# State scans: dt brought to the decay buffer by DMA, where TensorE spread it through PSUM

## The chip, the cores and the metric

The kernel runs on one core of one Trainium2 chip. The metric is the device time of one execution in microseconds (us), lower is better. The core has five engines with a queue of their own each: PE (TensorE, matmuls), DVE (VectorE), ACT (ScalarE), POOL (GpSimd) and SP (SyncE, which here only issues DMAs). ACT can issue DMAs too. Each queue is worked off in order; an instruction that waits for a semaphore holds up all that is queued behind it on its engine.

## The reference

A decoder of two layers over 4 sequences of 512 tokens with 512 features. What matters here are the two state-space (Mamba) mixers, `_L0_attn_ref` with 1024 channels and `_L1_xattn_ref` with 512, both with 16 states per channel:

```python
dt = jax.nn.softplus(jnp.einsum('blr,dr->bld', ts, dt_proj_w) + dt_proj_b)
A = -jnp.exp(A_log)

def step(h, inp):
    dt_t, B_t, C_t, x_t = inp
    dA = jnp.exp(dt_t[:, :, None] * A[None])
    h = dA * h + (dt_t * x_t)[:, :, None] * B_t[:, None, :]
    y = jnp.einsum('bdn,bn->bd', h, C_t)
    return (h, y)
...
x = _layernorm(x + _L0_attn_ref(x, ...))
x = _layernorm(x + _L0_xattn_ref(x, ...))
x = _layernorm(x + _L0_ffn_ref(x, ...))
x = _layernorm(x + _L1_attn_ref(x, ...))
x = _layernorm(x + _L1_xattn_ref(ctx_1024, x, ...))
x = _layernorm(x + _L1_ffn_ref(x, ...))
```

So every channel has one dt per token, and 16 decays dA = exp(dt * A), one for each state. Between the mixers stand a feed-forward net with 2048 hidden features (FFN) and a mixture of experts (MoE).

## The kernel before

Features lie on the 128 partitions, tokens (T = 512) along the free dimension. The sequences run one after another; the first `nc.Fori` body is repeated three times, and the last sequence has a copy of its own.

**A block of the scan.** `hidden_and_scan` handles 32 channels at a time, all with 16 states: 4 partition groups of 32 channels by 4 states (GRP) along the free dimension, so one block is a tile of 128 x 2048. A layer of 1024 channels has 32 blocks, one of 512 has 16. Per block s:

- PE, `spread_dt(s)` (L787): dt of 32 channels stands on 32 partitions. One float32 matmul with the constant `headmean` (four 32x32 identities side by side, divided by 16) copies it, over 16, to all 128 partitions of PSUM bank 0, `dt_bank`.
- ACT, `decays(s)` (L881): four exponentials read `dt_bank`, each with its own column of `rate` (A, multiplied by 16 at the start) as scale, and write the four quarters of the decay buffer `k.da[s % 2]`, 128 x 511 each. They wait for the matmul and, for the buffer, for the scan of block s - 2.
- PE, `spread_dtx(s)` (L799): the same spread for dt * x, into PSUM bank 1.
- DVE, `inputs(s)` (L912): dt * x times B, 128 x 2048, reads bank 1. `scan(s)` (L921): the recurrence over 2048 elements in one instruction; it waits for the decays and the inputs.
- POOL (L996): the states times C. PE, `reduce_quad` (L808): sums over the states, once per four blocks.

In the instruction records each of these float32 matmuls is two records (x2).

**What runs beside the scan.** The same function computes a hidden layer at the same time, one tile of 128 hidden features per step, and a step of the loop also holds one block of the scan. It is called in three ways:

- *first* (once, 32 blocks): no hidden layer. Beside the scan of the first sequence the weights are split into two bfloat16 parts (`WeightSplitter`): SP loads a slot of 768 KB (L211), ACT rounds it to the high part (L222), and the low part comes from DVE (L226) for every third slot, and for the others from PE (`rest_part`, L197 and L198) with a copy out of PSUM by ACT (`take_rest`, L203); SP then stores both parts (L214). 9 slots are handled in 4 steps; there are 4 buffers.
- *ffn* (4 times, 16 blocks of the second mixer, 16 tiles): gate, up and down products on PE (L258, L261, L262 are the three bfloat16 parts of one product), tanh on ACT (L888), the rest on DVE (L931, L939, L947, L244, L961).
- *moe* (3 times with 32 blocks of the next sequence's first mixer, 33 tiles; the fourth time without a scan).

**Order on the engines.** It is written out by hand. In a step of the loop PE has: `spread_dtx(step + 1)`, `spread_dt(step + 2)`, which waits until the decays of block step + 1 have read `dt_bank`, then gate and up of tile step + 1, the split's `rest_part`, `reduce_quad`, and a piece of the down product. ACT has: `decays(step + 1)`, tanh of tile step + 1, then the split's copies of the step. DVE has: `scan(step)`, the split's low part, `inputs(step + 1)`, and the tile's work. Ahead of the loop PE has `spread_dt(0)`, `spread_dtx(0)`, `gate(0)` (which waits for DVE's `xsplit`, four L244), `spread_dt(1)` and `up(0)`.

## Time and profile before

| | |
|---|---|
| device time, median of 3 runs | 4366.92 us (4363.65 to 4374.26) |
| device time of the profiled execution | 4378.06 us |
| its span, first to last instruction | 4376.3 us |
| PE busy | 3563.2 us, 81% |
| DVE busy | 3345.3 us, 76% |
| ACT busy | 1374.1 us, 31% |
| POOL busy | 1285.7 us, 29% |
| spread of dt and the decays, all of 192 blocks: PE L787 / ACT L881 busy | 232.5 / 463.2 us |
| mean granted TensorE clock | 0.884 of full speed |

The stretches with a scan in them are *first* (100 to 470 us), four times *ffn* (the first from 653 to 833 us) and three times *moe* (the first from 1118 to 1485 us). Read the busy shares with care. PE and DVE are both near full in some stretches, and an instruction counts as busy while it is held up by another engine. PE works on several row groups at once: matmuls of 32 rows that stand one behind the other in its queue can run together, and their busy times then cover the same stretch. What a stage costs is decided by the engine that has no idle time there, and by the waits that end last.

### The profile page before, as it was taken

Reading aid. Unit: us, or ns where it says so; the run is one execution under the profiler, and the core shown is the slowest. Engines: PE = TensorE matmul, PEld = TensorE weight load, DVE = VectorE, ACT = ScalarE, POOL = GpSimd, SP = SyncE. Lnnn points to the kernel's source line nnn. Section 1 sums busy time; section 2 is a strip of 40 time slices with the busy share of each in tenths; the row PEclk is TensorE's granted clock in tenths of the full one; section 3 lists DMA queues with packets and bytes.
Section 4 is the critical chain, followed back from the end, with each engine's and each line's share of the span. In section 5 each row is a group of like instructions: output and inputs, shape, how many; then the busy total and the mean of one; then the engine's idle time right before and its main releaser. Section 6 shows DMA issues by size and latency. Waiting matters only on the chain. (4 is left out here: it accounts for less than half of the span.)

```text
span 4376.3 us, 40273 instructions
## 1 busy us (share of the span) xinstructions
PE 3563.2 (81%) x14967; PEld 1484.2 (34%) x14967; DVE 3345.3 (76%) x2914; ACT 1374.1 (31%) x2022; POOL 1285.7 (29%) x452
## 2 busy tenths in 40 slices
PE   5777759887899859887899858978799967974898
PEld 1222233324333333323333333323333333321444
DVE  5998469777899768778799858868699868867444
ACT  4666333124322233214322233213422143221101
POOL 1543204332244203342244303333144312432000
PEclk9888879898899979989799978979799988986899
DMA  4888402221122302122122301122122311210222
GB/s 152 301 316 307 152 21 79 69 77 58 58 73 80 109 24 72 65 82 71 51 73 73 116 32 65 65 75 84 36 73 78 110 47 52 79 58 15 72 101 75
DMA packets 72917, 393.38 MB, mean 90 GB/s; under 512 B 8080, under 2 KB 8208, under 8 KB 70288
## 3 DMA queue, kind: packets, MB, share of 16 engines
q1 hardware_dynamic: 69264, 384.44, 25.1%
q10 hardware_dynamic: 3456, 6.29, 0.4%
q8 instruction: 126, 2.06, 0.2%
q14 instruction: 71, 0.58, 0.1%
HBM read 320.45 MB, written 70.25 MB: 89 GB/s over the span
## 5 line engine op out<-in xcount | busy, mean ns | idle before, releaser
L261 PE MATMUL ps<-r,ring 128*128 128x512 bf16 (+2 forms) x2040 | 801.2, 393 | 0.0
L996 POOL TENSOR_TENSOR hh<-hh,bc 128x2048 f32<-128x2048 f32 x72 | 336.9, 4679 | 1108.8 <-DVE hh L921 1108.8
L258 PE MATMUL ps<-r,ring 128*128 128x512 bf16 (+2 forms) x1384 | 557.5, 403 | 127.0 <-DVE xc L961 38.3
L258 PE MATMUL ps<-xr,ring 128*128 128x512 bf16 x1568 | 620.7, 396 | 5.5 <-DVE r L244 5.5
L262 PE MATMUL ps<-xr,ring 128*128 128x512 bf16 x1568 | 618.2, 394 | 0.0
L262 PE MATMUL ps<-r,ring 128*128 128x512 bf16 (+2 forms) x1384 | 556.4, 403 | 0.0
L881 ACT ACTIVATE da<-ps,params_sb 128x511 f32<-128x511 f32 x768 | 463.2, 690 | 72.7 <-PE ps L787 33.9
L996 POOL TENSOR_TENSOR bc<-bc 128x2048 f32<-128x2048 f32 x64 | 298.0, 4656 | 375.7 <-DVE bc L921 375.7
L996 POOL TENSOR_TENSOR r<-r,bc 128x2048 f32<-128x2048 f32 x56 | 261.8, 4674 | 327.8 <-DVE r L921 327.8
L921 DVE TENSOR_TENSOR_SCAN hh<-da,hh 128x2048 f32<-128x2048 f32 x72 | 326.7, 4538 | 1.5
L888 ACT ACTIVATE row<-ps 128x512 f32<-128x512 f32 x100 | 59.7, 597 | 754.5 <-PE ps L262 754.5
L921 DVE TENSOR_TENSOR_SCAN bc<-da,bc 128x2048 f32<-128x2048 f32 x64 | 289.6, 4525 | 0.5
L787 PE MATMUL ps<-r,squares_sb 32*128 32x512 f32 x384 | 232.5, 687 | 64.4 <-PEq L2026 49.6
L261 PEld LDWEIGHTS ps<-r,ring 128*128 128x128 bf16 (+2 forms) x2040 | 200.5, 98 | 248.7 <-issue 28.9
L258 PEld LDWEIGHTS ps<-r,ring 128*128 128x128 bf16 (+2 forms) x1384 | 136.8, 99 | 403.5 <-issue 265.9
L961 DVE TENSOR_TENSOR xc<-xc,ps 128x512 f32<-128x512 f32 x176 | 119.6, 680 | 198.9 <-PE ps L262 198.9
L258 PEld LDWEIGHTS ps<-xr,ring 128*128 128x128 bf16 x1568 | 153.5, 98 | 315.2 <-issue 141.5
L921 DVE TENSOR_TENSOR_SCAN r<-da,r 128x2048 f32<-128x2048 f32 x56 | 253.0, 4517 | 0.6
L888 ACT ACTIVATE r<-ps 128x512 f32<-128x512 f32 x96 | 57.3, 597 | 584.8 <-PE ps L262 584.8
L262 PEld LDWEIGHTS ps<-xr,ring 128*128 128x128 bf16 x1568 | 152.4, 97 | 211.5 <-issue 14.4
L197 PE MATMUL ps<-r,squares_sb 128*128 128x512 f32 x282 | 180.6, 727 | 53.1 <-ACT ring L222 20.3
L258 PE MATMUL ps<-bc,ring 128*128 128x512 bf16 (+2 forms) x320 | 139.2, 435 | 102.3 <-DMA ring<-wsplit 38.7
(240 smaller groups left out, 6486.9 us busy)
## 6 DMA issues: line engine op xcount, KB each, us to landing
ring<-wsplit SPq DMA_DIRECT2D x304, 768.0 KB, 4.2
r<-wstream SPq DMA_DIRECT2D x76, 768.0 KB, 7.4
wsplit<-ring SPq DMA_DIRECT2D x58, 768.0 KB, 4.9
wsplit<-r SPq DMA_DIRECT2D x18, 768.0 KB, 5.7
r<-xT SPq DMA_DIRECT2D x7, 1024.0 KB, 8.8
r<-gates_dram SPq DMA_DIRECT2D x3, 2048.0 KB, 8.3
bc<-guwT SPq DMA_DIRECT2D x4, 1024.0 KB, 12.1
out<-xr SPq DMA_DIRECT2D x4, 1024.0 KB, 7.0
```

The source lines that it names most:

```text
L197: pe.matmul(self.banks[:, c, :], ident, self.whole[n % SPLIT_RING][:, at], start=True, stop=False)
L258: mm = pe.matmul(out, w_hi, x_hi, start=start, stop=False)
L261: pe.matmul(out, w_hi, x_lo, start=False, stop=False)
L262: return pe.matmul(out, w_lo, x_hi, start=False, stop=stop)
L787: pe.matmul(dt_bank, k.headmean[at, :], dt[at, s // 4, :], start=True, stop=True).then_inc(dt_mm, 1)
L881: a = act.activation(k.da[s % 2][:, n, 1:T], dt_bank[:, 1:T], ACT.Exp, scale=rate[:, GRP * s + n:GRP * s + n + 1])
L888: act.activation(t2[jt % 2], gate_bank(jt), ACT.Tanh, scale=0.5).then_inc(th, 1)
L921: dve.tensor_tensor_scan(states(s), k.da[s % 2][:, :, :].rearrange("p n t -> p (n t)"), states(s), 0.0, ALU.mult, ALU.add).then_inc(scanne ...
L961: dve.tensor_tensor(k.xc[:, m, :], k.xc[:, m, :], down_bank(p), ALU.add).then_inc(taken, 1)
L996: pool.tensor_tensor(quartet(s), quartet(s), k.out_rows, ALU.mult).then_inc(read, 1)
```

## The change

dt reaches the four partition groups by DMA. A new `fetch(s)` on ACT's queue issues four DMAs (L871 of the changed kernel), each from the 32 partitions of dt to one group of 32 partitions in the first quarter of `k.da[s % 2]`, 32 x 511 float32 (65 KB). The four exponentials (L878) read that quarter; the one that overwrites it comes last, and waits until the other three have read it. `spread_dt`, its matmuls, the waits between it and the decays, and `dt_bank` go. The factor 16 in the rates goes with them.

`fetch(s)` for s >= 2 waits for the scan of block s - 2, as the decays did before, since the buffer is free only then. It stands in step s - 2, behind the decays and the tanh, and ahead of the split's copies. `fetch(0)` and `fetch(1)` stand at the start.

```diff
-        dt_mm, dtx_mm, decay = [sem(n) for n in ("dt_mm", "dtx_mm", "decay")]
+        dtx_mm, decay, others = [sem(n) for n in ("dtx_mm", "decay", "others")]
+        dt_in = [sem(f"dt_in{i}") for i in range(2)]
...
-            def spread_dt(s):
-
-                if s >= 1:
-                    pe.wait_ge(decay, s)
-                at = slice(32 * (s % 4), 32 * (s % 4) + 32)
-                pe.matmul(dt_bank, k.headmean[at, :], dt[at, s // 4, :], start=True, stop=True).then_inc(dt_mm, 1)
...
             if blocks:
-                spread_dt(0)
                 spread_dtx(0)
             if tiles:
                 pe.wait_ge(xsplit, KM)
                 gate(0)
-            if blocks:
-                spread_dt(1)
...
                     spread_dtx(step + 1)
-                if step + 2 < blocks:
-                    spread_dt(step + 2)
...
-            def decays(s):
-                act.wait_ge(dt_mm, s + 1)
+            def fetch(s):
+
                 if s >= 2:
                     act.wait_ge(scanned, s - 1)
-                for n in range(GRP):
-                    a = act.activation(k.da[s % 2][:, n, 1:T], dt_bank[:, 1:T], ACT.Exp, scale=rate[:, GRP * s + n:GRP * s + n + 1])
+                rows = dt[32 * (s % 4):32 * (s % 4) + 32, s // 4, 1:T]
+                for g in range(4):
+                    act.dma_start(k.da[s % 2][32 * g:32 * g + 32, 0, 1:T], rows).then_inc(dt_in[s % 2], 16)
+
+            def decays(s):
+                act.wait_ge(dt_in[s % 2], 64 * (s // 2 + 1))
+                for n in (1, 2, 3, 0):
+                    if n == 0:
+                        act.wait_ge(others, s + 1)
+                    a = act.activation(k.da[s % 2][:, n, 1:T], k.da[s % 2][:, 0, 1:T], ACT.Exp,
+                                       scale=rate[:, GRP * s + n:GRP * s + n + 1])
+                    if n == 3:
+                        a.then_inc(others, 1)
                 a.then_inc(decay, 1)
...
             if blocks:
+                fetch(0)
+                fetch(1)
                 decays(0)
...
                 if step + 1 < tiles:
                     gate_tanh(step + 1)
+                if step + 2 < blocks:
+                    fetch(step + 2)
                 for n, late in zip_longest(split_now(step), split_now(step, 2)):
...
-            dve.tensor_scalar(k.a0, k.a0, -16.0, None, ALU.mult)
-            dve.tensor_scalar(k.a1, k.a1, -16.0, None, ALU.mult).then_inc(neg, 1)
+            dve.tensor_scalar(k.a0, k.a0, -1.0, None, ALU.mult)
+            dve.tensor_scalar(k.a1, k.a1, -1.0, None, ALU.mult).then_inc(neg, 1)
```

ACT's queue in *first*, around step 3. L203 is `take_rest`, L222 the high part of a slot. Before:

```order
L881 ACTIVATE da<-ps,params_sb 128x511 [waits first_scanned,first_dt_mm]
L881 ACTIVATE da<-ps,params_sb 128x511 x3
L203 ACTIVATE ring<-ps 128x1536 [waits first_rest]
L222 ACTIVATE ring<-r 128x1536 [waits first_stored2,first_landed2]
L203 ACTIVATE ring<-ps 128x1536 [waits first_rest]
L222 ACTIVATE r<-r 128x1536 [waits first_stored3,first_landed3]
L222 ACTIVATE ring<-r 128x1536 [waits first_stored0,first_landed0]
```

With the change, at the same place:

```order
L878 ACTIVATE da<-da,params_sb 128x511 [waits first_dt_in0]
L878 ACTIVATE da<-da,params_sb 128x511 x2
L878 ACTIVATE da<-da,params_sb 128x511 [waits first_others]
L871 DMA da<-r 32x511 [waits first_scanned]
L871 DMA da<-r 32x511 x3
L203 ACTIVATE ring<-ps 128x1536 [waits first_rest]
L222 ACTIVATE ring<-r 128x1536 [waits first_stored2,first_landed2]
L203 ACTIVATE ring<-ps 128x1536 [waits first_rest]
L222 ACTIVATE r<-r 128x1536 [waits first_stored3,first_landed3]
L222 ACTIVATE ring<-r 128x1536 [waits first_stored0,first_landed0]
```

The wait for a scan has moved from ahead of the decays to behind them, and it is now one for the scan of this step (3), not of the one before (2). The five copies of the split stand behind it.

PE's queue in *first*, one step. Before:

```order
L799 MATMUL ps<-dtx_now,squares_sb 128x512 [waits first_dtx_in,first_inp]
L787 MATMUL ps<-r,squares_sb 128x512 [waits first_decay]
L197 MATMUL ps<-r,squares_sb 128x512 [waits first_low_act,first_high]
L198 MATMUL ps<-ring,r 128x512
L197 MATMUL ps<-r,squares_sb 128x512
```

With the change:

```order
L793 MATMUL ps<-dtx_now,squares_sb 128x512 [waits first_dtx_in,first_inp]
L197 MATMUL ps<-r,squares_sb 128x512 [waits first_low_act,first_high]
L198 MATMUL ps<-ring,r 128x512
L197 MATMUL ps<-r,squares_sb 128x512
```

L787 is gone, and with it PE's wait for ACT's decays ahead of the split's products.

PE's queue at the start of *ffn*; the semaphores there are used again and carry the names of their first use (`first_stored3` is `xsplit`, `first_landed2` is `decay`). Before, with the nine products between left out as they do not change:

```order
L787 MATMUL ps<-r,squares_sb 128x512
L799 MATMUL ps<-r,squares_sb 128x512
L258 MATMUL ps<-xr,ring 128x512 [waits w_landed0,first_stored3]
...
L262 MATMUL ps<-xr,ring 128x512
L787 MATMUL ps<-r,squares_sb 128x512 [waits first_landed2]
L258 MATMUL ps<-xr,ring 128x512 [waits w_landed0]
```

With the change:

```order
L793 MATMUL ps<-r,squares_sb 128x512
L258 MATMUL ps<-xr,ring 128x512 [waits w_landed0,first_stored3]
...
L262 MATMUL ps<-xr,ring 128x512
L258 MATMUL ps<-xr,ring 128x512 [waits w_landed0]
```

`spread_dt(0)` ahead of `spread_dtx(0)` and `spread_dt(1)` between gate and up of tile 0 are gone.

## Rows read from the trace of the kernel before

**Rows 1.** Windows: the first ffn and moe; us, busy per engine, PEclk, DMA, GB/s.
```profile
655.00:850.00 195.00, 177.17 (x799) 70.20 (x798) 170.27 (x120) 53.60 (x90) 74.78 (x17) 0.96 0.23 77
1120.00:1485.00 365.00, 341.34 (x1571) 128.67 (x1570) 347.81 (x258) 95.10 (x161) 147.02 (x32) 0.98 0.23 76
```

**Rows 2.** Groups by line: busy us, mean ns of one, idle before and releaser.
```profile
L881 ACT ACTIVATE da<-ps,params_sb 128x511 f32<-128x511 f32 x768 | 463.2, 690 | 72.7 <-PE ps L787 33.9 <-DVE bc L921 20.0 <-DVE r L921 14.1
L787 PE MATMUL ps<-r,squares_sb 32*128 32x512 f32 x384 | 232.5, 687 | 64.4 <-PEq L2026 49.6 <-ACT da L881 9.3 <-PEq L421 5.4
...
L1448 ACT ACTIVATE da<-r 128x511 f32<-128x511 f32 x32 | 17.0, 614 | 0.0
```

**Rows 3.** Timeline in moe, PE: start us, duration us; a pair of spreads.
```profile
1383.89 0.69 PE L799 MATMUL ps<-dtx_now,squares_sb 32*128 32x512 f32 x1
...
1383.89 0.69 PE L787 MATMUL ps<-r,squares_sb 32*128 32x512 f32 x1
...
1384.95 0.40 PE L258 MATMUL ps<-xr,ring 128*128 128x512 bf16 x1
```

**Rows 4.** Timeline near the end of ffn, PE: a spread of dtx alone.
```profile
801.58 1.12 PE L799 MATMUL ps<-r,squares_sb 32*128 32x512 f32 x2
```

**Rows 5.** Timeline in moe: decays of block 74, and the scan of block 74.
```profile
1388.59 2.42 ACT L881 ACTIVATE da<-ps,params_sb 128x511 f32<-128x511 f32 x4 [0.17 <-DVE hh L921]
...
1404.93 4.42 DVE L921 TENSOR_TENSOR_SCAN bc<-da,bc 128x2048 f32<-128x2048 f32 x1
```

**Rows 6.** Timeline at the start of the first ffn, PE and DVE.
```profile
653.37 2.50 DVE L244 TENSOR_TENSOR r<-xr 128x512 bf16<-128x512 f32 x4 [1.88 <-PEq L2026]
...
657.05 0.61 PE L258 MATMUL ps<-xr,ring 128*128 128x512 bf16 x1
...
662.28 1.23 PE L787 MATMUL ps<-r,squares_sb 32*128 32x512 f32 x2
...
663.44 0.40 PE L258 MATMUL ps<-xr,ring 128*128 128x512 bf16 x1
...
667.37 2.29 DVE L912 TENSOR_TENSOR hh<-ps,bc 128x2048 f32<-128x2048 f32 x1 [3.39 <-PE ps L799]
```

**Rows 7.** Timeline at the start of the first moe, DVE.
```profile
1132.20 2.29 DVE L912 TENSOR_TENSOR hh<-ps,bc 128x2048 f32<-128x2048 f32 x1 [2.89 <-PE ps L799]
```

**Rows 8.** The DMAs that ACT issues before: issue ns min/median/max, and landing.
```profile
L1460 ACTq DMA_DIRECT2D gates_dram<-r x12: 326/326/353, 975.6 to 2997.7; - x12
...
DMA to landing us min/median/max: 2.0/2.0/5.3
```

**Rows 9.** Timeline in first, steps 3 and 4, DVE.
```profile
140.67 1.73 DVE L226 TENSOR_TENSOR ring<-r,ring 128x1536 bf16<-128x1536 f32 x1
142.32 2.28 DVE L912 TENSOR_TENSOR r<-ps,bc 128x2048 f32<-128x2048 f32 x1
144.70 6.37 DVE L921 TENSOR_TENSOR_SCAN r<-da,r 128x2048 f32<-128x2048 f32 x1
151.92 5.40 DVE L226 TENSOR_TENSOR ring<-r,ring 128x1536 bf16<-128x1536 f32 x1 [0.85 <-ACT ring L222]
...
187.84 6.36 DVE L921 TENSOR_TENSOR_SCAN bc<-da,bc 128x2048 f32<-128x2048 f32 x1
```

**Rows 10.** The same stretch, POOL and ACT.
```profile
151.15 4.56 POOL L996 TENSOR_TENSOR r<-r,bc 128x2048 f32<-128x2048 f32 x1 [4.36 <-DVE r L921]
...
143.87 1.47 ACT L222 ACTIVATE ring<-r 128x1536 bf16<-128x1536 f32 x1
```

**Rows 11.** Timeline in first, second half: PE, ACT, and two scans four steps apart.
```profile
349.88 4.42 DVE L921 TENSOR_TENSOR_SCAN r<-da,r 128x2048 f32<-128x2048 f32 x1
...
352.77 2.07 PE L787 MATMUL ps<-r,squares_sb 32*128 32x512 f32 x2 [2.28 <-ACT da L881]
...
360.25 1.45 ACT L203 ACTIVATE ring<-ps 128x1536 bf16<-128x1536 f32 x1 [6.17 <-PE ps L198]
...
396.12 4.41 DVE L921 TENSOR_TENSOR_SCAN bc<-da,bc 128x2048 f32<-128x2048 f32 x1
```

2 lines of the change are left out of this document (1 added, 1 removed).

## The prediction, made before the changed kernel was run

> **What bounds the kernel now.** I read the windows by stage first, then the groups by line, then the timeline of one step in each kind of stage. In the first ffn and moe windows DVE is busy 170 of 195 us and 348 of 365, and PE 177 and 341 [rows 1]: both look full, so either could be the bound, and the 232.5 us that PE is busy with the spread of dt [rows 2] look like up to 5% of the time. The timeline says otherwise. The spreads of dtx and of dt stand next to each other in PE's queue and use different 32-row groups of the array. In moe both start at 1383.89, and the next product starts at 1384.95, 1.06 us later [rows 3]. At the end of ffn a spread of dtx that stands alone takes 1.12 us [rows 4]. The pair costs what one costs. Within the loop, then, the dt spread is nearly free on PE, and it is DVE's queue of scan, inputs and tile work that sets the step of ffn and moe.
>
> **Part 1, the spread leaves PE in the loop of ffn and moe.** By rows 3 against rows 4 the gain per step is about 0, at most some 0.4 us in the few steps where the two spreads do not start together. DVE would hide even that. I take 0 us. Ends: 0, and a gain of some 20 us if 0.2 us of each of the 112 later steps of PE (of 160) were on the path.
>
> **Part 2, ACT gets the DMAs and a wait.** Per block: four issues at 0.33 us if a 32-row issue costs what a 128-row issue of ACT costs [rows 8], and perhaps a third of that if it goes by rows; I take 1.0 us for four and call it f, with 0.4 to 1.4 as ends. The data lands 2.0 us after the last issue in quiet, 5.3 us beside a big load [rows 8]. The four exponentials take 2.42 us [rows 5]; the last now also waits for the third to finish, some 0.1 us. In moe the decays of block 74 start at 1388.59 and are done at 1391.0, and the scan that needs them starts at 1404.93 [rows 5]: 13.9 us in hand. The new chain adds f + 2.0 to 5.3 us + 0.1, so 3.1 to 6.8 us. Behind the waiting instructions on ACT stands only the tanh of the next tile, which is needed after that same scan. Cost in the loop of ffn and moe: 0 us; if the 13.9 us were not there, each step would pay the 3 us or more, 160 times.
>
> The exponentials now read SBUF. The one line of ACT that does so at this shape takes 614 ns, against 690 from PSUM [rows 2]: 192 x 4 x 0.076 = 58 us less on ACT, beside other work. The Trainium skill says the opposite (Perfetto Trace Analysis, Optimizing Scalar/DVE Operations): ScalarE's access overhead is about 93 ns on SBUF and 51 on PSUM, which by that page would be 768 x 0.042 = 32 us more. As ACT has slack in most stages, the sum is the same by either.
>
> **Part 3, the start of ffn and moe.** Here PE is late. `inputs(1)` waits 3.39 us for PE in ffn [rows 6] and 2.89 us in moe [rows 7]. Ahead of it on PE stand dt(0), dtx(0), gate(0), dt(1), up(0), dtx(1). Without dt(0), gate(0) can start when `xsplit` is done at 653.37 + 2.50 = 655.87, where it started at 657.05 [rows 6]: 1.2 us. Without dt(1), up(0) follows at once: 663.44 - 662.28 = 1.2 us [rows 6]. Some comes back: the products take 0.61 us before and 0.40 us after the clock has risen [rows 6], and if it rises no sooner, three or four of the up products run at the slow level, 0.2 us each. Net 1.7 us for ffn. In moe `xsplit` comes later behind the first `dtx_now`, so I take 1.4 us. Bounds: 0 and the whole idle time, 3.39 and 2.89 us. The decays of block 0 come from the DMA now: eight issues are 2f, the fourth lands 0.75f + 2.0 us after the start, and scan 0 moves by less than 1 us either way. Its end is still ahead of the new start of `inputs(1)`. DVE has no idle time in the rest of the loop, so what it gains here it keeps until the end of the stage, whose tail hangs on the last scan. Gain: 4 x 1.7 + 3 x 1.4 = 11 us (0 to 22).
>
> **Part 4, first.** Here ACT's order matters. DVE and POOL exclude each other for some of these instructions. Scan 4 starts at 144.70 and takes 6.37 us [rows 9], where 4.42 is normal [rows 5], since POOL is still at work; and the low part at 151.92 takes 5.40 us where the one at 140.67, which came before POOL's instruction, takes 1.73 [rows 9]. POOL started at 151.15 and ended at 155.71 [rows 10], and the low part ended 1.6 us after that. So it counts whether a low part is ready at once when a scan ends. Before, ACT ran ahead: it did the high part during the scan. Now the split's copies of step s stand behind `fetch(s + 2)`, which waits for the end of scan s. A low part that needs the high part of the same step (two of the three in four steps) can start f + 1.35 + 1.4 = 3.8 us after the scan's end at the soonest; a copy takes 1.47 us [rows 10]. By then POOL has the ports until 4.6 us. So both such steps look like the one at 151.92. From scan end to scan end that is 4.6 + 1.65 + 2.2 + 4.4 = 13 us (POOL, low part, inputs, scan). The one with the low part at 140.67, which starts as scan 3 ends, took until 144.70 + 6.37 = 151.07, so 10.4 us: +2.6 us in four steps. ACT itself now needs, in a step with five copies, f + 5 x 1.4 + 2.3 for decays, plus waits for PE's rest and for a load that could not be issued sooner: some 14 to 14.5 us against 13, which adds another 1.0. The four steps that took 187.84 - 144.70 = 43.1 us [rows 9] should take 46.7. That pace held for the first 17 steps: 3.5 groups x 3.6 = +12.6 us.
>
> In the second half the four steps already take 396.12 - 349.88 = 46.2 us [rows 11]. There PE's dt spread waits for ACT's decays (2.28 us at 352.77), the split's products stand behind it, and ACT waits 6.17 us for those at 360.25 [rows 11]. That ring is cut by the change, and the wait for the scan comes in its place: 46.2 against 46.7, so I take 0 us, with -12 (back to 43.1) and +15 (50) as ends.
>
> At the start of first, the copy of slot 0 now waits for scan 0, and DVE's low part of slot 0 stands ahead of scan 1: f + 1.47 = 2.5 us, plus 1 us for a dt that lands beside four loads of 768 KB: +3.5 us. The last steps have no fetch.
>
> **Sum.** 0 + 0 - 11 + 12.6 + 0 + 3.5 = +5 us. On the profiled execution, 4378.06 us, that is 4383; it lies 11 us above the median of the three runs, and its own span leaves under 2 us outside. On the median of 4366.92 it is 4372 us.
>
> **Rivals.**
> - *A, ACT becomes the pace of first (slower).* If four issues take 2.5 us or more instead of 1.0, or dt lands later than 8 us after the scan because each DMA engine first serves the queue of the big loads, ACT's queue from scan end to scan end is longer than DVE's 13 and 9 us. It decides when f plus landing plus decays exceeds about 11 us. With 50.5 us per four steps, 3.8 us more for 7 groups, it gives +27 us: 4399. For it: 5.3 us of landing beside one load [rows 8], and first has three in flight. Against: the copies (4 to 7 us) hide most of the landing.
> - *B, the starts gain nothing.* If dt(0) lands so late that scan 0 moves back by 2 us, or the later clock takes all, the 11 us fall away: +16, 4383 us.
> - *C, first gets faster.* If the cut ring in rows 11 counts and ACT keeps up, the second half goes back to 43.1 us: 3.5 x 3.1 = -11, and the first half costs half as much: +5 - 11 - 6 = -12, or 4355; with the full idle time of part 3 gained too, 4344.
> - *D, PE's busy time was on the path after all.* 0.5 us or more per step: -80 us. Rows 3 against rows 4 speak against it.
>
> **How the numbers follow.** Forecast 0.5 (4356 to 4384), A 0.15, B 0.15, C 0.17, D 0.03. The range has to hold A's milder half, B and C: 4344 to 4397. What can be told from no change here is about 0.3%, 13 us. Faster by more than that: D, half of C and the low tail of the forecast, 0.18. Slower by more: A, most of B and the high tail, 0.32. Within: 0.50.
>
> **What would show it right or wrong.** In the profile after: the spread of dtx alone costs PE 1.06 to 1.12 us per step, as the pair did. `inputs(1)` in ffn waits under 2.5 us. The steps of ffn and moe after the second keep their length. In first a fetch starts right at each scan's end, low parts that start 3 to 5 us after a scan's end and end after POOL, and four steps take 46 to 47 us in both halves. If first is longer by over 30 us, A holds. If ffn or moe steps change at all in the middle of a stage, parts 1 and 2 are wrong.

## The result and the profile after

| | before | after |
|---|---|---|
| device time, median (lowest to highest, 4 runs each) | 4365.28 us (4362.22 to 4374.26) | 4426.79 us (4417.00 to 4434.02) |
| ratio after / before | | 1.0136, 95% interval 1.0118 to 1.0154 |
| device time of the profiled execution | 4378.06 us | 4417.00 us |

The changed kernel is slower by 1.4%, 61.5 us at the median, and lies outside the range that was given. The profiled execution of before was its slowest and that of after its fastest, so the two traces show only 39 us. A later profile of the kernel before (4361.1 us of span) is the better partner and is used below; it is called *the second profile of before*.

The page of after: the span, the busy line of the engines, the new DMA queue (packets, MB, share of the DMA engines), and the groups of the exponentials and of the first form of the scan.

```profile
span 4415.2 us, 39870 instructions
...
PE 3500.8 (79%) x14338; PEld 1465.2 (33%) x14583; DVE 3309.9 (75%) x2914; ACT 1430.2 (32%) x2022; POOL 1278.3 (29%) x452
...
q10 hardware_dynamic: 40320, 56.58, 5.0%
...
L878 ACT ACTIVATE da<-da,params_sb 128x511 f32<-128x511 f32 x768 | 511.5, 713 | 637.1 <-DMA da<-r 630.7
...
L925 DVE TENSOR_TENSOR_SCAN hh<-da,hh 128x2048 f32<-128x2048 f32 x72 | 321.9, 4471 | 38.5 <-ACT da L878 37.9
```

An exponential takes 713 ns from SBUF, against 690 from PSUM [rows 2]. The 630.7 us for which ACT waits for the transfers look like the loss, but most of that is a wait beside other work. Where it reaches DVE is in the last line: 37.9 us over all scans of this form, in eight waits, one at the start of each stage.

The same windows as in [rows 1], moved by the shift of each stage (busy us of PE, PEld, DVE, ACT, POOL; granted clock, DMA share, GB/s):

```profile
689.00:884.00 195.00, 176.09 (x756) 69.72 (x768) 169.46 (x118) 58.39 (x90) 73.20 (x16) 0.95 0.31 95
1157.00:1522.00 365.00, 336.12 (x1477) 128.07 (x1505) 348.98 (x259) 105.88 (x162) 146.76 (x32) 0.97 0.33 99
```

DVE's busy time there is that of before within 1.2 us. In ffn and moe the loop is as it was. The stages, worked out from the traces, us. A stage's begin is here the start of its first vector instruction (`dtx_now` or `xsplit`), which the change leaves alone. The first spread of dtx would be a false mark: before, it stands behind `spread_dt(0)`, 1.84 us after the begin in every stage, and in the changed kernel it is the first product in its queue.

| stretch | before, second profile | after |
|---|---|---|
| first: begin to end of the last scan | 355.0 | 402.2 |
| of it: begin to scan 0 / scan 0 to the end of the last scan | 6.2 / 348.8 | 12.7 / 389.5 |
| last scan of first to the begin of ffn | 194.9 | 187.5 |
| ffn, begin to end of the last scan, four times | 159.7 each | 160.8, 159.8, 159.4, 160.3 |
| moe, the same, three times | 342.9 each | 344.2, 344.5, 344.6 |

That is +47.2 us in first, +1.7 in the four ffn, +4.5 in the three moe, and +0.7 in all the rest (-7.4 right behind first), which sums to the 54.1 us between the two spans (4415.2 and 4361.1). The loss is in first. Its second half loses too: from scan end to scan end, groups of four steps take 50.3, 47.9, 49.1, 53.5, 51.1, 52.2 and 48.2 us after, and 43.1, 43.1, 43.1, 46.4, 47.2, 46.2 and 45.1 before.

What the issues cost, first as the trace of after has it: ACT's DMA instructions, ns min/median/max, with who waited for them and the time to landing.

```profile
L871 ACTq DMA_DIRECT2D da<-r x768: 513/612/1727, 99.5 to 3834.7; - x192
...
  ACT da L878: 630.7, 157
...
DMA to landing us min/median/max: 1.9/2.0/8.3
```

And one row of the kernel before, SP's queue at the start of first, which the prediction did not use: four issues in a row, 2.48 us (0.33, 0.43, 0.42 and 1.15 us, with small gaps).

```profile
99.97 2.48 SPq L211 DMA_DIRECT2D r<-wstream  x4
```

Four issues in a row took 2.44 us in the quietest steps of after and 2.64 us on average in first, up to 4.41 us beside SP's own issues. The row of before was a warning that four can take 2.5 us, but not a price for these: it is another queue with transfers of 768 KB, and half of its length is the last issue. The 326 ns of [rows 8] are those of an issue that stands alone, and of another transfer. In the changed kernel the first of four takes 0.51 us and each that follows at once 0.61.

One step of first in the changed kernel (start us, duration us, and in brackets the idle time before and what ended it):

```profile
204.82 1.76 DVE L226 TENSOR_TENSOR r<-r 128x1536 bf16<-128x1536 f32 x1 [5.40 <-ACT r L222]
...
206.49 2.28 DVE L916 TENSOR_TENSOR bc<-ps,bc 128x2048 f32<-128x2048 f32 x1
...
208.88 4.42 DVE L925 TENSOR_TENSOR_SCAN bc<-da,bc 128x2048 f32<-128x2048 f32 x1
...
211.15 2.68 ACT L878 ACTIVATE da<-da,params_sb 128x511 f32<-128x511 f32 x4
...
213.34 2.84 ACTq L871 DMA_DIRECT2D da<-r  x4
...
216.22 1.45 ACT L203 ACTIVATE ring<-ps 128x1536 bf16<-128x1536 f32 x1 [2.38 <-issue]
...
217.57 1.47 ACT L222 ACTIVATE ring<-r 128x1536 bf16<-128x1536 f32 x1
...
219.07 1.76 DVE L226 TENSOR_TENSOR ring<-r,ring 128x1536 bf16<-128x1536 f32 x1 [5.77 <-ACT ring L222]
```

Scan 8 ends at 213.30. ACT's queue then issues for 2.84 us, the engine stands idle for 2.38 of them ("issue"), takes a rest, makes the high part, and only at 219.07 can DVE start the low part: 5.77 us of DVE's time. This is what the whole stage shows. DVE's waits for the high part in first, us in total, times, longest; two lines of the second profile of before, then two of after.

```profile
DVE ring L226 <- ACT ring L222: 17.1, 8, 5.5
DVE r L226 <- ACT r L222: 6.4, 3, 4.7
```

```profile
DVE ring L226 <- ACT ring L222: 68.2, 12, 8.2
DVE r L226 <- ACT r L222: 24.3, 5, 7.0
```

23.5 us became 92.5. Not all of the 69 us is lost, since DVE's instructions are shorter when they do not meet POOL's: the scan above takes 4.42 us and not 6.37 [rows 9], and the low part 1.76 and not 5.40. Over the stage DVE's busy time fell from 321.9 to 284.5 us.

TensorE's granted clock in the stage is 0.83 of full speed after and 0.87 before, both of them a mean over its two levels (1.2 and 2.4 GHz), and a product of the split (L197, L198) takes 675 ns instead of 626. In the runs below the clock is 0.79 to 0.86 where the stage is longer than 360 us, and 0.87 or 0.88 where it is shorter. It moves with the loss; how much of the loss goes through it no run separates.

### The profile page after: what moved, and what is told of

It is laid out like the page before. It is cut to its first block and busy times, and to the rows that moved or that the text cites. A ratio compares the mean times of both kernels' runs of the same rounds, so it can differ in the third digit from the quotient of the medians.

```text
span 4415.2 us, 39870 instructions
## 1 busy us (share of the span) xinstructions
PE 3500.8 (79%) x14338; PEld 1465.2 (33%) x14583; DVE 3309.9 (75%) x2914; ACT 1430.2 (32%) x2022; POOL 1278.3 (29%) x452
## 5 line engine op out<-in xcount | busy, mean ns | idle before, releaser
L261 PE MATMUL ps<-r,ring 128*128 128x512 bf16 (+1 forms) x2023 | 796.4, 394 | 41.0 <-POOL r L244 14.6
L878 ACT ACTIVATE da<-da,params_sb 128x511 f32<-128x511 f32 x768 | 511.5, 713 | 637.1 <-DMA da<-r 630.7
L258 PE MATMUL ps<-r,ring 128*128 128x512 bf16 (+2 forms) x1326 | 534.1, 403 | 107.2 <-DVE xc L965 38.5
L262 PE MATMUL ps<-xr,ring 128*128 128x512 bf16 x1549 | 613.9, 396 | 0.9 <-issue 0.4
L258 PE MATMUL ps<-xr,ring 128*128 128x512 bf16 x1496 | 595.7, 398 | 3.3 <-DVE r L244 2.1
L262 PE MATMUL ps<-r,ring 128*128 128x512 bf16 (+2 forms) x1362 | 546.4, 402 | 0.7
L1000 POOL TENSOR_TENSOR r<-r,bc 128x2048 f32<-128x2048 f32 x56 | 258.1, 4610 | 342.2 <-DVE r L925 342.2
L925 DVE TENSOR_TENSOR_SCAN hh<-da,hh 128x2048 f32<-128x2048 f32 x72 | 321.9, 4471 | 38.5 <-ACT da L878 37.9
L261 PEld LDWEIGHTS ps<-r,ring 128*128 128x128 bf16 (+2 forms) x2040 | 201.6, 99 | 251.6 <-issue 33.4
L197 PE MATMUL ps<-r,squares_sb 128*128 128x512 f32 x282 | 193.6, 776 | 107.0 <-ACT ring L203 46.3
L258 PEld LDWEIGHTS ps<-r,ring 128*128 128x128 bf16 (+2 forms) x1384 | 136.5, 99 | 400.6 <-issue 260.4
L793 PE MATMUL ps<-dtx_now,squares_sb 32*128 32x512 f32 x256 | 152.3, 676 | 87.5 <-DVE dtx_now L920 56.8
L262 PEld LDWEIGHTS ps<-r,ring 128*128 128x128 bf16 (+2 forms) x1384 | 136.4, 99 | 194.1 <-issue 27.3
```

Source lines behind the costliest of these rows:

```text
L197: pe.matmul(self.banks[:, c, :], ident, self.whole[n % SPLIT_RING][:, at], start=True, stop=False)
L258: mm = pe.matmul(out, w_hi, x_hi, start=start, stop=False)
L261: pe.matmul(out, w_hi, x_lo, start=False, stop=False)
L262: return pe.matmul(out, w_lo, x_hi, start=False, stop=stop)
L793: pe.matmul(dtx_bank, k.headmean[at, :], source, start=True, stop=True).then_inc(dtx_mm, 1)
L878: a = act.activation(k.da[s % 2][:, n, 1:T], k.da[s % 2][:, 0, 1:T], ACT.Exp, scale=rate[:, GRP * s + n:GRP * s + n + 1])
```

## The experiments

The theory after the first look, called A as in the prediction: ACT is the pace of first, through the wait for the scan and the length of the issues ahead of the split's copies. Rivals: the transfers themselves (landing, traffic), the order alone, the starts of the later stages. The column "first" is from the start of scan 0 to the end of the last scan in the profiled execution; "DVE waits" is its waiting for high parts in first; "own wait" is a wait of ACT's queue for ACT's own last exponentials, right ahead of the issues; the ratio is to the kernel before on the same chip.

| run | on ACT in first, per step | first | DVE waits | whole, median | ratio, 95% |
|---|---|---|---|---|---|
| c0_before | nothing new | 348.8 | 23.5 | 4363.95 | 1.001 (1.000 to 1.002) |
| after | wait for the scan, 4 issues | 389.5 | 92.5 | 4426.79 | 1.0136 (1.0118 to 1.0154) |
| e1_wait_only | the wait | 373.2 | 53.4 | 4384.87 | 1.005 (1.0035 to 1.0066) |
| e4_one_dma | the wait, 1 issue | 367.3 | 60.3 | 4390.86 | 1.0065 (1.0048 to 1.0082) |
| e8_issues_only | own wait, 4 issues | 389.1 | 88.7 | 4419.19 | 1.0134 (1.0115 to 1.0152) |
| e10_one_no_wait | own wait, 1 issue | 348.1 | 20.4 | 4385.66 | 1.0066 (1.0046 to 1.0085) |
| e11_idle_transfers | own wait, 4 issues that nobody needs | 391.2 | 91.9 | 4410.33 | 1.0108 (1.0090 to 1.0126) |
| e9_copies | 4 copies, no issue | 369.9 | 61.5 | 4394.01 | 1.0079 (1.0062 to 1.0096) |
| e13_under_exps | 4 issues, one behind each exponential | 350.6 | 29.8 | 4376.03 | 1.0024 (1.0010 to 1.0038) |
| e12_one_by_one | the wait, 4 issues between the copies | 379.8 | 80.2 | 4408.71 | 1.0093 (1.0066 to 1.0121) |
| e2_fetch_last | copies, then wait and 4 issues | 457.0 | 124.8 | 4491.38 | 1.0283 (1.0265 to 1.0300) |
| e3_first_by_pe | nothing new | 343.9 | 20.6 | 4365.28 | 1.0004 (0.9995 to 1.0014) |
| e5_by_sp | nothing; SP issues | 367.3 | 59.1 | 4367.68 | 1.0014 (1.0004 to 1.0025) |
| e6_mixed | nothing; SP issues | 364.0 | 57.5 | 4374.12 | 1.0025 (1.0015 to 1.0035) |
| e7_before_early | nothing new | 347.7 | 23.0 | 4361.17 | 0.9989 (0.9978 to 1.0000) |
| e14_best | as e13_under_exps | 347.0 | 34.1 | 4353.94 | 0.9973 (0.9960 to 0.9986) |

Three things limit what the columns can tell. Identical code gave 1.001. A first stage that works the same way in all of them measured 352.0, 348.8, 343.9 and 347.7 us (the first profile, c0_before, e3_first_by_pe, e7_before_early). So differences of some 0.1% of the whole and of up to 8 us of the stage are not read here. And a stage is known from one execution only, which can lie well off the median: that of e1_wait_only was the slowest of its runs (13 us above it), that of e10_one_no_wait the fastest (11 us below).

### Where in the program: the first stage by TensorE again (e3_first_by_pe)

```diff
+        by_pe = splitter is not None
...
+                if by_pe and step + 2 < blocks:
+                    spread_dt(step + 2)
...
+                if by_pe:
+                    return
```

> The changed kernel with the first stage alone as before: there TensorE spreads dt and the decays read PSUM; in the ffn and moe stages dt comes by transfers. Theory A (all of the loss lies in the first stage, the later ones are even: the first scan of each comes 2.3 to 3.2 us later and its second step is 2.1 to 2.8 us shorter): 4363 to 4372, the kernel before within 0.2%. Rival S (the loss is also in the starts of the seven later stages and shows only after first): 4380 to 4395.

Measured 4365.28 us, 1.0004 of before. Without the change in the first stage the loss of 61.5 us is gone. The ffn and moe stages are changed as in after, and they are nearly even: 159.4 to 159.9 us against 159.7, and 343.6 against 342.9, which makes +2.3 us over all seven.

### The wait alone, and the wait with one issue (e1_wait_only, e4_one_dma)

e1_wait_only is the kernel before with:

```diff
+                if step + 2 < blocks:
+                    act.wait_ge(scanned, step + 1)
```

> This is the kernel before (TensorE spreads dt, decays read PSUM) with one thing of the change alone: ScalarE waits for scan(step) behind gate_tanh(step + 1) and ahead of the splitter's copies, at the place of the fetch, and issues no transfer. Theory A, as sharpened by the trace of the changed kernel (in the first stage ScalarE sets the pace, since the wait for the scan and then the four issues stand ahead of the copies that the splitter's low parts on VectorE wait for): the wait holds the copies until the scan's end but costs no ScalarE time of its own, so the first stage grows by a part of the 38 us only, 5 to 20 us: 4370 to 4385. Rival L (only the length of the issues, 2.4 us a block, counts; a wait alone would have been over by then): 4365, within 3 us. Rival W (the wait alone does it): +30 or more, 4395 to 4405.

e4_one_dma is the changed kernel with:

```diff
-                for g in range(4):
-                    act.dma_start(k.da[s % 2][32 * g:32 * g + 32, 0, 1:T], rows).then_inc(dt_in[s % 2], 16)
+                act.dma_start(k.da[s % 2][:, 0, 1:T], dt[:, s // 4, 1:T]).then_inc(dt_in[s % 2], 16)
```

> The changed kernel with one transfer of 128 rows for each block in place of four of 32 rows: the same bytes into the same rows of the decay buffer, but each partition gets its own row of dt and not its block's head, so dt and with it the decays are other numbers. It varies the number of issues alone (3 x 0.6 = 1.8 us less of ScalarE a block), the wait and its place stay. Theory A with the issues' length as the main term: of the +38 us of the first stage (30 blocks behind the start) 15 to 35 come back, and the starts of the later stages come 1.8 us earlier (7 x 1.8 = 13): 4375 to 4395. Rival W (the wait's place does it, not its length): 4405 to 4420. Rival D (landing time or DMA load): 4415 to 4430, since the bytes are the same.

The wait alone costs the first stage 24 us and the whole 22 (4384.87 against 4362.58), with no ACT time of its own: it keeps the high parts from being made during the scan. The single issue of 128 rows takes 0.47 us, carries the same number of bytes as the four, and adds nothing to that (367 against 373 us). It leaves out the repetition of a block's 32 rows, so every partition gets its own row of dt and the decays are other numbers; the work is the same. So neither the bytes nor the exponentials from SBUF make the rest of the loss; the number of issues does.

### The issues without the wait (e8_issues_only, e10_one_no_wait)

In first the transfers go to rows of the residual's tile, free there, so they need no wait for the scan. They got another one: right ahead of the issues ACT's queue waits for its own last exponentials, those of the block before. It is stricter than it need be, since the rows were last read two blocks before:

```diff
-                if s >= 2:
+                if s >= 2 and not splitter:
                     act.wait_ge(scanned, s - 1)
...
+                    to = k.xr[:, s % 2, :] if splitter else k.da[s % 2][:, 0, :]
+                    act.dma_start(to[32 * g:32 * g + 32, 1:T], rows).then_inc(dt_in[s % 2], 16)
...
                 if step + 2 < blocks:
+                    if splitter:
+                        act.wait_ge(decay, step + 2)
                     fetch(step + 2)
```

> The changed kernel, but in the first stage dt lands in rows of the residual's tile, which are free there, so that ScalarE's four issues a block need no wait for the scan and stand right behind the decays of the block before, ahead of the splitter's copies. It is the counterpart of the run that had the wait alone (4385). Theory A2 with the two costs separate: the issues alone give 5 to 20 us, 4370 to 4385, since ScalarE is then only busier by 2.4 us a step and early enough. If the issues' length counts fully even without the wait (ScalarE's queue sets the pace by its own work): 4395 to 4415. If the wait alone made the loss and the issues only lengthen it where they follow it: 4365 to 4370.

e10_one_no_wait is that with, in first (again every partition gets its own row of dt):

```diff
+                if splitter:
+                    act.dma_start(k.xr[:, s % 2, 1:T], dt[:, s // 4, 1:T]).then_inc(dt_in[s % 2], 16)
+                    return
```

> As the run with the four issues and no wait, but in the first stage one transfer of 128 rows in place of four of 32 (each partition gets its own row of dt and not its block's head, so dt is other numbers there): 0.47 us of ScalarE a block in place of 2.44, and no wait for the scan. Theory T: the first stage is nearly that of the kernel before, 345 to 358 us; with the later stages even and the start of the first 5 us later 4366 to 4378. If the transfers' bytes or their landing cost, it stays near 380 to 390 us and 4400 to 4415.

The expectation for four issues fell: without the wait they cost as much as with it, 389.1 against 389.5 us. The two costs are not a sum. With one issue, and the own wait still there, the stage is back at 348.1 us, that of before: the own wait alone costs nothing that can be seen. This holds for the profiled execution, which was the fastest of four and spans 4372.4 us; the whole at the median, 4386, is 26 us above before and above what was expected. What makes the other executions slower is open. This stage also has no spread of dt on TensorE, and is no faster for it.

### Is it ACT's time, or the transfers? (e9_copies, e11_idle_transfers)

Both are the kernel before, spread and all, with something added in first at the place of the fetch:

```diff
+                    for n in range(4):
+                        a = act.activation(k.xr[:, n, 1:431], dt[:, (step + 2) // 4, 1:431], ACT.Copy)
```

> The kernel before, with nothing of the change: in the first stage ScalarE makes four copies of 128 x 430 a step (about 0.6 us each, 2.4 together) into free rows, at the place where the changed kernel issues its four transfers. No transfer and no wait for the scan. Theory T (ScalarE's time ahead of the splitter's copies is what costs): the first stage grows as in the run with the issues and no wait, by 30 to 45 us: 4395 to 4410. Theory Q (the loss comes with the transfers themselves, by their landing or by what they take from the queues and engines that the splitter's own transfers use): 4365 to 4380.

```diff
+                    act.wait_ge(decay, step + 2)
...
+                    for g in range(4):
+                        act.dma_start(k.xr[32 * g:32 * g + 32, s % 2, 1:T],
+                                      dt[32 * (s % 4):32 * (s % 4) + 32, s // 4, 1:T]).then_inc(dt_in[s % 2], 16)
```

> The kernel before, with TensorE's spread kept and used; in the first stage ScalarE also issues the four transfers of dt a step into free rows that nobody reads, without a wait for the scan. Beside the run with four copies of the same length it tells the issues from the transfers. Theory T: the same as that run within 5 us, 4395 to 4410. Theory Q: 10 us or more above it. Rival L (what cost was that the exponentials wait for the landing, 3.9 to 9 us, where TensorE's spread took 1.1): 4370 to 4385, since nobody waits for these.

The added instructions, ns min/median/max, in the one and in the other:

```profile
L903 ACT ACTIVATE xr<-r x120: 571/583/621, 107.9 to 453.9; 128x430 f32<-128x430 f32 x120
```

```profile
L906 ACTq DMA_DIRECT2D xr<-r x120: 514/614/1568, 108.2 to 475.2; - x120
```

Transfers that nobody reads cost the stage the whole loss, 391.2 us. So it is not that somebody waits for their landing. Copies cost 21 us and issues 42, and the expectation that both would be equal fell. Part of it is length: four copies overlap and take 1.94 us from the first start to the last end, 58 us in 30 steps; four issues take 2.81 us, 84 us. Per us of ACT that is 0.36 and 0.50. The rest was open, and led to the next pair.

### Issues under running activations (e13_under_exps, e12_one_by_one)

In the trace of e2_fetch_last an issue ran while the activation ahead of it was still executing. The thought was that four issues in a row behind one activation can hide a piece of the first alone, and that one issue behind each of four activations might be hidden whole. e13_under_exps is e8_issues_only with the same four transfers moved in between the exponentials that stood ahead of them. The own wait moves too: it stands ahead of the exponentials and is for those of the step before:

```diff
                     for n in range(GRP):
                         a = act.activation(k.da[s % 2][:, n, 1:T], k.xr[:, s % 2, 1:T], ACT.Exp,
                                            scale=rate[:, GRP * s + n:GRP * s + n + 1])
+                        if s + 1 < blocks:
...
+                            fetch(s + 1, [n])
```

> As the run with the four issues and no wait for the scan (first stage 389 us from its first scan to its last), but in the first stage each of the four issues for block s + 1 stands behind one of the four exponentials of block s, so that it can run while the exponential executes (0.51 to 0.61 us beside 0.71). The same transfers, bytes, landing and users. Theory T2 (what costs is that ScalarE stands idle during a row of issues): the first stage goes back to 345 to 358 us, and the whole to 4375 to 4390 (the later stages are those of the changed kernel, and the first scan of the first stage comes 3 to 5 us late). Rival D (the transfers themselves cost, by landing or traffic): 375 us or more, 4400 or more.

A step of it. The four issues (2 and 2) run under the copies ahead of the exponentials and end under the second exponential, and the next copy follows without a gap for "issue":

```profile
208.05 1.45 ACT L203 ACTIVATE ring<-ps 128x1536 bf16<-128x1536 f32 x1 [2.27 <-PE ps L198]
...
208.61 1.16 ACTq L872 DMA_DIRECT2D xr<-r  x2
...
209.40 1.48 ACT L222 ACTIVATE r<-r 128x1536 bf16<-128x1536 f32 x1
...
209.83 2.05 ACTq L872 DMA_DIRECT2D xr<-r  x2
...
210.77 2.54 ACT L882 ACTIVATE da<-xr,params_sb 128x511 f32<-128x511 f32 x4
...
213.22 1.47 ACT L222 ACTIVATE ring<-r 128x1536 bf16<-128x1536 f32 x1
```

The first stage takes 350.6 us, from 389.1. Same bytes, same number of issues, same engine, same users. The spacing is not what helps: here too the four issues of a step follow each other within 0.1 us, and with 103 us in sum they are longer than the 80 us of e8_issues_only. But ACT's queue had already handed copies and exponentials to the engine when it came to them. Of those 103 us the engine was executing in 95; in e8_issues_only and e11_idle_transfers, where the first issue starts 0.03 us after the last exponential has ended, in none of 80 and 82 us. In after it is 11 of 77 us. The idle time of ACT that the issues ended, in first: of after, then of e13_under_exps.

```profile
ACT ring L222 <- issue: 29.2, 7, 7.5
ACT ring L203 <- issue: 22.3, 9, 4.1
ACT r L222 <- issue: 10.5, 3, 3.6
ACT r L203 <- issue: 7.2, 4, 1.9
```

```profile
ACT ring L203 <- issue: 4.5, 3, 2.4
ACT r L203 <- issue: 2.1, 2, 1.5
ACT da L882 <- issue: 1.6, 4, 0.9
```

69 us against 8. This is the cause, shown and not only argued: ACT's engine stood idle while its queue issued, because a wait right ahead of the issues had let it run out of work. Four issues in a row behind handed-over work, and without the own wait in e8_issues_only, were not run by themselves; e2_fetch_last (below) comes near, with 70 of its 81 us of issues covered by the copies ahead of them. The whole is still 11 us above before, since the starts stayed: scan 0 of first comes 6.5 us late, and the seven later stages are 6.7 us longer together.

e12_one_by_one keeps the wait and the decay buffer, and puts one issue ahead of the copies and one behind each of three:

```diff
                         splitter.high_part(act, n)
+                        if left:
+                            fetch(step + 2, [left.pop(0)])
```

> The changed kernel, in the first stage with the wait for the scan kept, but only the first of the four issues ahead of the splitter's copies and one more behind each of the next three. Theory T2: three of the four issues are hidden under copies, so the stage falls from 389 us towards the 367 to 373 us that the wait costs with one issue or none, if the later landing does not make the next exponentials late; in the run with the fetch behind all copies they were late by 6 us a step. With the landing half hidden 370 to 395 us, the whole 4400 to 4430. If it is above 400 us, the landing outweighs what is hidden.

379.8 us, as expected halfway: 63 of 67 us of issues are covered now, and ACT's exponentials wait 46.7 us for the later landing in first.

### The order alone (e2_fetch_last)

```diff
-                if step + 2 < blocks:
-                    fetch(step + 2)
                 for n, late in zip_longest(split_now(step), split_now(step, 2)):
...
+                if step + 2 < blocks:
+                    fetch(step + 2)
```

> The changed kernel with the fetch of step + 2 moved behind the splitter's copies of the step, so that high parts and taken rests no longer stand behind the wait for the scan and the four issues. The issues still cost ScalarE 2.4 us a block. Theory A: DVE's low parts find their high parts as early as before, and the first stage gives back most of its +38 us, unless the next decays, now right behind the issues and 3.9 us of landing, come late for the scan of step + 2 (they do not follow until decays(step + 1) of the next step, so the landing has a whole step): 4385 to 4400 (26 to 41 us below the changed kernel). If ScalarE's busy time in the stage is what counts and not the order, the time stays at 4415 to 4430. Rival D (the landing of the transfers beside the first stage's own traffic is what counts): unchanged or slower, since they are issued later.

Measured 4491.38 us, 65 us above the changed kernel, and the expectation was wrong in a plain way: the next thing on ACT behind that fetch is `decays(step + 2)`, which needs its data at once, not a step later. The transfer is issued at 243.03 and 244.21, the exponentials start at 252.09, and the scan waits for them:

```profile
242.65 1.45 ACT L203 ACTIVATE ring<-ps 128x1536 bf16<-128x1536 f32 x1 [3.92 <-PE ps L198]
...
243.03 1.16 ACTq L871 DMA_DIRECT2D da<-r  x2
...
244.00 1.48 ACT L222 ACTIVATE r<-r 128x1536 bf16<-128x1536 f32 x1
...
244.21 1.97 ACTq L871 DMA_DIRECT2D da<-r  x2
...
252.09 2.69 ACT L878 ACTIVATE da<-da,params_sb 128x511 f32<-128x511 f32 x4 [6.61 <-DMA da<-r]
...
254.81 4.42 DVE L925 TENSOR_TENSOR_SCAN r<-da,r 128x2048 f32<-128x2048 f32 x1 [4.59 <-ACT da L878]
```

In first the last data lands 7.1 to 10.4 us after the first issue in 23 of 30 steps. In the changed kernel the copies cover that. They cannot stand both ahead of the issues and behind them.

### SyncE as the issuer (e5_by_sp), block 0 by TensorE (e6_mixed)

```diff
+            for step in range(blocks - 2):
+                if tiles:
+                    k.w.load_until(sp, slot + step + 2, RING - 1, last)
+                fetch(step + 2)
+                for n in split_now(step, 1):
+                    next(moves)
```

> The changed kernel with the same four transfers a block, issued by SyncE in place of ScalarE: SyncE waits for scan(step) and issues them, and its weight loads and the splitter's loads and stores of each step stand behind them. ScalarE keeps the exponentials alone. Theory A2 (the loss of the first stage is made on ScalarE's queue: the wait for the scan ahead of the splitter's copies gives about 20 of it, the length of four issues about 36): both go, and the stage takes 345 to 355 us from its first scan to its last, as with TensorE's spread; with its start (+5) 4362 to 4375. Rival D (the traffic or the landing is what costs): 4390 or more. Rival Q (SyncE's queue becomes the late one: the splitter's stores stand 2.4 us later behind a wait, and the high parts wait for buffers): 4375 to 4390, with ScalarE's copies waiting for transfers.

e6_mixed adds to that, with a copy of the first rates times 16 for block 0:

```diff
             if blocks:
+                pe.matmul(dt_bank, k.headmean[0:32, :], dt[0:32, 0, :], start=True, stop=True).then_inc(dt_mm, 1)
                 spread_dtx(0)
...
+            if blocks:
+                spread_dtx(1)
             if tiles:
                 up(0)
```

> As the run with the transfers on SyncE, but block 0 of every stage gets dt from TensorE's spread as in the kernel before, and the spread of dtx for block 1 stands ahead of the product up(0). Theory: the first scan comes 4.35 us behind the stage's begin, as before, and the second scan no longer waits for up(0) (2.3 to 2.8 us in each of the seven later stages): 7 x 2.5 = 17 us below the kernel before, and nothing lost in the first stage: 4343 to 4355. Rival Q (SyncE's queue late in the first stage): 4355 to 4375. Rival S (the second scan then waits for its decays, since dt of block 1 lands 3.9 us or more after the begin): 4355 to 4368.

The first stage gives back 22 to 26 of its 41 us and no more. What took their place is, by the waits, rival Q: the loads of the split stand behind the fetch on SP's queue, and the high parts wait for them. The exponentials wait for dt there too, 20.8 and 21.9 us. In first, e6_mixed, then the second profile of before:

```profile
ACT ring L236 <- DMA r<-wstream: 38.0, 30, 4.2
```

```profile
ACT ring L222 <- DMA r<-wstream: 5.9, 8, 1.2
```

The ffn and moe stages gain when SP issues: 157.5 us against 159.7, and 341.8 to 342.2 against 342.9, which makes 11.4 us over the seven. With block 0 by TensorE and the early spread of dtx they take 157.1 and 340.7 to 340.8 us, 16.6 us less in all.

### The start without any transfer (e7_before_early)

```diff
             if blocks:
                 spread_dt(1)
+                spread_dtx(1)
             if tiles:
                 up(0)
```

> The kernel before with one reordering and no transfer: TensorE's spread of dtx for block 1 stands ahead of up(0) in place of behind it. If the seven later starts gain because inputs(1) no longer stands behind up(0), and not because dt comes by transfers, the second scan starts 2.3 to 2.8 us earlier in each: 4343 to 4352. If the gain belongs to the transfers: 4360 to 4368. The first stage has no up(0) and stays as it was (344 to 352 us from its first scan to its last).

`inputs(1)` at the first moe waits 0.24 us where it waited 2.89 [rows 7]:

```profile
1122.78 2.29 DVE L913 TENSOR_TENSOR hh<-ps,bc 128x2048 f32<-128x2048 f32 x1 [0.24 <-PE ps L799]
```

Each stage is shorter by 2.0 to 2.2 us, with no transfer at all, which makes 15 us; the whole gained 3, within what identical code shows. In its trace the stretches between the stages are longer: ffn to moe 307.2 us against 305.6, and moe to ffn 194.2, 188.0 and 190.8 against 188.6, 188.6 and 185.0. Of the last, 2.9 us are the wait at the first layer norm of a sequence, behind the block that clears the semaphores. Behind a moe it is between 14.6 and 22.5 us long in all traces; here in the second profile of before and in e7_before_early:

```profile
3548.00 2.48 DVE L1054 TENSOR_TENSOR xc<-ps,r 128x512 f32<-128x512 f32 x4 [15.06 <-PEq L2026]
```

```profile
3547.53 2.48 DVE L1055 TENSOR_TENSOR xc<-ps,r 128x512 f32<-128x512 f32 x4 [17.94 <-PEq L2027]
```

Whether an earlier end of the stage makes that wait longer or chance does, two traces cannot tell.

### The second profile of before, and all findings together (c0_before, e14_best)

> The kernel before itself, for a second profile of it: the one that stands with the times of before was its slowest execution (4378.06 against a median of 4365.28). The block that clears the semaphores between two sequences makes VectorE wait 13 to 22 us at the first layer norm in every profile, in steps of about 3 us, and the first stage has measured 344 to 352 us from its first scan to its last where its code is the same. Every theory expects 4364 within 5 us, with a first stage of 342 to 350 us.

4363.95 us, and a first stage of 348.8: the second profile of before.

e14_best is e6_mixed for ffn and moe. In first SP has the split's transfers alone, as before, and ACT issues under the exponentials, into free rows:

```diff
+            def bring(s, g):
+                act.dma_start(k.xr[32 * g:32 * g + 32, s % 2, 1:T],
+                              dt[32 * (s % 4):32 * (s % 4) + 32, s // 4, 1:T]).then_inc(dt_in[s % 2], 16)
...
+                    for n in range(GRP):
+                        a = act.activation(k.da[s % 2][:, n, 1:T], k.xr[:, s % 2, 1:T], ACT.Exp,
+                                           scale=rate[:, GRP * s + n:GRP * s + n + 1])
...
+                        if s + 1 < blocks:
+                            bring(s + 1, n)
```

> All findings together: block 0 of every stage by TensorE's spread; in the first stage ScalarE's issues one behind each exponential, into free rows, so without a wait for the scan; in the ffn and moe stages SyncE issues, and the spread of dtx for block 1 stands ahead of up(0). First stage 343 to 353 us from its first scan to its last; the seven later ones 2.2 to 2.5 us shorter each, of which the reordered kernel before kept only 3 us in the whole time. Theory T2: 4355 to 4366, at most 0.2% below the kernel before. Rival D: 4380 or more.

4353.94 us at the median of 12 runs, 0.9973 of the kernel before (0.9960 to 0.9986). It beats both kernels, before by 0.27% and after by 1.6%. The first stage is that of before (353.1 us from its begin, against 355.0), the later ones are 157.1 and 340.8 to 340.9 us. So a form of the idea that is no loss exists, but all that it wins lies in the starts: 16.1 us over the seven stages, where e7_before_early has 14.6 without a transfer. Why the whole gained 11 us here and 3 there is not shown.

## Why the prediction was wrong

**The step that failed is f in part 2.** Four issues were put at 1.0 us, with 0.4 and 1.4 as ends. They took 2.44 us at the least and 2.64 on average in first. The error was to take the price of an issue from rows of single issues of another transfer [rows 8], and to guess that a 32-row issue costs a third. The length does not go by rows: 0.47 us for one of 128 rows, 0.51 for the first of four with 32 and 0.61 for each that follows. The one row of before with four in a row, 2.48 us on SP, was not looked for.

**Part 4, by its own logic, was right in kind.** It said that low parts start at f + 1.35 + 1.4 = 3.8 us after the scan's end. With f = 2.5 that is 5.3 us; the step above shows 5.77. With that the first three full groups took 47.9 to 50.3 us and not 46.7. The 0 for the second half was wrong: those groups took 48.2 to 53.5 us against 45.1 to 47.2. Over the seven groups that is +38.1 us where +12.6 was forecast. The start of first was forecast at +3.5 and came to +9.1: scan 0 comes 6.5 us later (eight issues and a table load, and then 3.1 us of waiting for dt, where 1 was forecast), and the steps up to scan 3 take 2.6 us more.

**Rival A was what happened.** Its condition, four issues of 2.5 us or more, is met, and its pace of 50.5 us per four steps is the measured one: 50.3 on average. It was given 0.15. Its +27 us stand on top of the forecast's +12.6, so it had 39.6 us for the seven groups, where 38.1 were measured. Even so its 4399 us is 28 us short, and the range ended below it, at 4397. What A lacked too is the rest of the sum: it kept the -11 us of the seven starts, which came to +6.2, and the +3.5 of the start of first, which came to +9.1; and the loss at the median is 7 us more than between the two traces. Of A's two conditions the landing was not the one: e11_idle_transfers has the loss with data that nobody waits for, and e13_under_exps loses nothing although its data lands 9.1 us after the first issue on average, against 6.1 in after.

**Part 1 held.** PE's spread of dt had cost nothing in the loop: DVE's busy time and the scans' spacing in ffn and moe stayed, the lone spread of dtx takes 1.12 us in after as in [rows 4], and first without the spread (e10_one_no_wait) is no faster. Rival D is out, and so is C.

**Part 2 on the loop of ffn and moe held**; the exponentials' size did not: 713 ns and not 614. The row of 614 ns [rows 2] is of another form: its exponentials have a constant scale (-1.0), where the decays take theirs from a column of `rate`. The Trainium skill (Perfetto Trace Analysis, Optimizing Scalar/DVE Operations) had the sign right against the row that the prediction went by, with 42 ns between SBUF and PSUM. From the start of one exponential to the start of the next these traces show 613 ns after and 569 before, so they agree; the durations differ by 23. It did not matter for the time.

**Part 3 was right about PE and wrong about ACT.** `inputs(1)` no longer waits for PE, as was said, and where SP issues the transfers the seven stages do gain 11.4 us (e5_by_sp), the forecast's 11. That the two figures are so near is luck, for its terms were rounded from two starts. With ACT's issues scan 0 was to move by less than 1 us and moved by 2.3 to 3.9 us. At the first moe, the second profile of before (the table load stands in the wait for PE) and after (it stands behind eight issues):

```profile
1113.63 1.28 ACT L881 ACT_TABLE_LOAD   x1 [12.59 <-PEq L2026]
...
1115.76 2.42 ACT L881 ACTIVATE da<-ps,params_sb 128x511 f32<-128x511 f32 x4 [0.84 <-PE ps L787]
...
1119.87 4.42 DVE L921 TENSOR_TENSOR_SCAN hh<-da,hh 128x2048 f32<-128x2048 f32 x1
```

```profile
1157.06 5.71 ACTq L871 DMA_DIRECT2D da<-r  x8
...
1162.79 1.28 ACT L878 ACT_TABLE_LOAD   x1 [18.34 <-issue]
...
1164.09 2.70 ACT L878 ACTIVATE da<-da,params_sb 128x511 f32<-128x511 f32 x4
...
1166.82 4.42 DVE L925 TENSOR_TENSOR_SCAN hh<-da,hh 128x2048 f32<-128x2048 f32 x1 [4.43 <-ACT da L878]
```

5.71 + 1.28 + 2.70 = 9.7 us from the begin to scan 0, against 6.2 before. The second step gives back 2.5 us in ffn and 2.0 in moe. The sum had -11 us for the seven starts; the stages came out at +6.2 us together. Once f is 2.5, 2f = 5 us stands in the prediction's own formula, so this too is mostly the same term. The table load was not thought of.

## What to carry to other kernels

Price an issue from a row with the same kind of transfer, and with as many in a row as the change will put there. Then look at what stands ahead of it in the queue. Behind instructions that the engine still has to work off, even four issues in a row were hidden for the most part; behind a wait for the engine's own results or for another engine's, they left it idle for nearly their whole length. So if a compute engine must issue transfers, put them between its long instructions, and give the data a buffer of its own so that no wait stands right ahead of them. And before an engine that is 31% busy is given work, look at the stage in which its results are waited for last: in first ACT was busy 67% of the time before the change (235 of 349 us), and there 1.9 us of copies a step cost 0.7 us a step.

## What the runs showed of the hardware

- One issue on ACT: 0.47 us with 128 rows of 511 float32, 0.51 with 32 rows; the ones that follow at once 0.61 each, with 32 rows. Single ones grew to more than 1 us, 2.7 at most. All four of these in the first stage of after, and all 33 in that of e13_under_exps, stand beside an issue of SP or start less than 3 us behind one; of the shorter ones 34 of 116 and 56 of 87 do. The Trainium skill (Perfetto Trace Analysis, DMA Instruction — HWDGE) says that the two issuing queues share one block that makes the descriptors and that the profiled time holds the wait for it; these lengths agree.
- ACT's queue issues while its engine executes what was handed to it before: 95 of 103 us of issues in the first stage of e13_under_exps, with 8 us of idle time left, against 69 us in after, where they stand behind a wait.
- An exponential of 128 x 511 float32 takes 713 ns from SBUF and 690 from PSUM; from start to start it is 613 and 569.
- The time from the first of four issues to the last landing was 4.1 us on average in ffn and moe and 6.1 us in first, where the DMA engines are busy at 84% of the time and more.
- The first layer norm behind a moe waits 14.6 to 22.5 us behind the block that clears the semaphores, the same code from one execution to the next. What sets its length is open.
